# Second target for the scatter-adds: each slot's two blocks go to x_rows and y_rows, summed in the last graph stage

## What is computed

```python
x = x + _L0_gnn_ref(_layernorm(x), adj, W, b)       # A @ (ln @ W + b) / degree
x = x + _L0_ffn_ref(_layernorm(x)[None], ...)[0]    # 8 experts, top 2, 256 -> 1024 -> 256, gelu
x = x + _L1_gnn_ref(_layernorm(x), adj, W, b)       # relu(normalised (A + I) @ ln @ W.T + b)
x = x + _L1_ffn_ref(_layernorm(x)[None])[0]         # shifts of one-hot nibbles, elementwise per row
```

## Time and profile before

| what | value |
|---|---|
| median of 3 runs | 1076.81 us |
| the profiled execution's own time | 1077.18 us |
| its span on the core | 1075.2 us |
| PE busy | 956.4 us, 89% of the span |
| DVE / ACT / POOL busy | 559.4 / 404.4 / 360.0 us |
| second block, first work to last | 348.3 to about 794 us |
| last matmul of the second block, first of the third | 777.05 / 802.32 us |
| adds into `x_rows` (L1064) | 76, mean 1.604 us on POOL |
| read and written in memory | 176.41 and 22.94 MB |

### The profile page before, as it was taken

The page is one execution under the profiler, slowest core; times in us unless marked ns, Lnnn a source line. Parts: engine busy times, 40 slices in busy tenths (PEclk is TensorE's granted clock), DMA queues, the critical chain, the costliest instruction groups (busy, mean ns, idle before and its releaser), DMA issues. The chain is left out here.

```text
span 1075.2 us, 22179 instructions
## 1 busy us (share of the span) xinstructions
PE 956.4 (89%) x6724; PEld 627.4 (58%) x6725; DVE 559.4 (52%) x1643; ACT 404.4 (38%) x826; POOL 360.0 (33%) x416
## 2 busy tenths in 40 slices
PE   4988999999922799999999999999819999999993
PEld 1444544444411689898989898898704454444541
DVE  6734113127598566565656565665436334161754
ACT  4863758676787233232323232323112101010111
POOL 3510000014575345454545455454425320110110
PEclk9999999999965799999999999999959999999997
DMA  9785898899786423232332323232259978876771
GB/s 346 307 293 186 287 328 319 312 345 371 257 278 183 156 41 55 45 54 45 50 50 45 54 43 56 40 55 44 46 161 393 406 254 298 291 240 189 231 254 35
DMA packets 91265, 200.00 MB, mean 186 GB/s; under 512 B 13328, under 2 KB 47120, under 8 KB 91088
## 3 DMA queue, kind: packets, MB, share of 16 engines
q1 hardware_dynamic: 69248, 164.17, 43.5%
q0 software_dynamic: 17792, 31.02, 14.6%
q10 hardware_dynamic: 4176, 4.19, 1.2%
HBM read 176.41 MB, written 22.94 MB: 185 GB/s over the span
## 5 line engine op out<-in xcount | busy, mean ns | idle before, releaser
L921 PE MATMUL bank<-adj_f,feat 128*128 128x512 f16 x1024 | 240.8, 390 | 17.4 <-DMA adj_f<-in_adjT 15.7
L1202 ACT ACTIVATE act_f<-bank,b_sb 128x256 f32<-128x256 f32 x304 | 127.6, 471 | 288.4 <-PE bank L1148 288.4
L1148 PE MATMUL bank<-rT,experts 128*128 128x256 f16 x1824 | 207.8, 275 | 0.9 <-DVE rT L1215 0.9
L1169 PE MATMUL bank<-experts,act_h 128*128 x1824 | 205.3, 273 | 1.4 <-DVE y_f L1247 1.4
L1148 PEld LDWEIGHTS bank<-rT,experts 128*128 x1824 | 179.5, 98 | 22.9 <-issue 1.2
L1169 PEld LDWEIGHTS bank<-experts,act_h 128*128 128x128 f16 x1824 | 176.8, 98 | 21.6 <-issue 1.7
L1064 POOL DMA_INDIRECT x_rows<-y,token x76 | 121.9, 1604 | 193.1 <-DVE y L1254 165.2
L921 PEld LDWEIGHTS bank<-adj_f,feat 128*128 128x128 f16 x1024 | 97.5, 96 | 144.4 <-issue 18.1
L1588 PE MATMUL bank<-adj_g,feat 128*128 128x512 f16 x768 | 179.7, 387 | 0.3 <-POOL feat L1393 0.3
L805 ACT ACTIVATE spent<-adj_f 128x1024 f16<-128x1024 f32 x128 | 135.1, 1055 | 33.5 <-DMA adj_f<-in_adjT 28.3
L1588 PEld LDWEIGHTS bank<-adj_g,feat 128*128 128x128 f16 x768 | 73.8, 96 | 94.1 <-issue 0.8
(11 more groups left out here) (258 smaller groups left out, 910.0 us busy)
## 6 DMA issues: line engine op xcount, KB each, us to landing
adj_f<-in_adjT SPq DMA_DIRECT2D x128, 512.0 KB, 6.7
adj_g<-in_adjT SPq DMA_DIRECT2D x72, 512.0 KB, 6.0
adj_early<-in_adjT SPq DMA_DIRECT2D x24, 512.0 KB, 6.6
adj_g<-in_adjT SPq DMA_DIRECT2D x48, 256.0 KB, 3.1
unit_f<-in_W SPq DMA_DIRECT2D x16, 512.0 KB, 7.3
stage<-in_W SPq DMA_DIRECT2D x12, 512.0 KB, 7.0
x_ring<-in_x POOLq DMA_DIRECT2D x16, 256.0 KB, 7.6
x_rows<-agg SPq DMA_DIRECT2D x4, 1024.0 KB, 9.6
```

Of the source, the lines that this page charges most:

```text
L921: last = pe.matmul(mine(s)[ib * DC + c][:, :], feat0[:, j, h, c * P:(c + 1) * P], adj_0[j % RING][:, ib * HALF_SWEEP:(ib + 1) * HALF_SWEEP ...
L1148: last = pe.matmul(pb[2 + q][:, k * SLOT:(k + 1) * SLOT], w1_part(e * DC + (f // FQ * W2_UNIT0 + c), wh)[:, (f % FQ) * P:(f % FQ + 1) * P] ...
L1169: last = pe.matmul(pb[6 + r][:, 0:D], act_h[i][:, ah, f, r * P:(r + 1) * P], experts[:, ds(e * DC + (W2_UNIT0 + f // UH), 1), wh, (f % UH) ...
L1202: last = a.activation(act_f[q][:, k, :], pb[2 + q][:, k * SLOT:(k + 1) * SLOT], ACT.Gelu, bias=b1_sb[:, ds(e * FC + (2 * q + k), 1)], scal ...
```

## The change

The two blocks of a slot get a tensor each. Block 0 is added into `x_rows` as before, block 1 into a new tensor `y_rows`, which the first block fills with zeros (32 stores of 128 KB from `zeros_f`, a tile of zeros which takes the place of the unused `xn`). Each of the two has a semaphore of its own. Both adds of a slot are issued one behind the other, ahead of the gathers, and both are waited for at the end of the slot, before the next slot's adds. In the third block each piece is loaded from both tensors (y into a ring of 16 tiles, `y_ring`), and DVE adds y to x before the statistics.

```diff
@@ first block, SP
+            sp.wait_ge(sem("zrow_set"), 2)
+            for k in range(T // P):
+                sp.dma_start(y_rows[k * P:(k + 1) * P, :], zeros_f[:, :]).then_inc(sem("mix_stored"), 16)
             sp.wait_ge(sem("mix_ready"), 1)
             sp.dma_start(ln_rows[0:T, D:ROW].rearrange("(n p) d -> p n d", p=P), mix[:, :, :]
                          ).then_inc(sem("mix_stored"), 16)
...
-            sp.wait_ge(sem("mix_stored"), 16)
+            sp.wait_ge(sem("mix_stored"), 16 * (1 + T // P))
@@ first block, POOL
+            pool.memset(zeros_f[:, :], 0.0).then_inc(sem("zrow_set"), 1)
@@ second block, POOL
             def add_rows(i, r):
-                pool.indirect_dma_start(x_rows[:, :], ...
-                                        y[i][:, r, :], None, compute_op=ALU.add).then_inc(sem("landed"), 16)
+                pool.indirect_dma_start(sum_of[r][:, :], ...
+                                        y[i][:, r, :], None, compute_op=ALU.add).then_inc(sem(f"landed{r}"), 16)
-            def landed_until(s, r):
-                pool.wait_ge(sem("landed"), (s * SR + r) * 16 + 16)
+            def landed_until(s):
+                for r in range(SR):
+                    pool.wait_ge(sem(f"landed{r}"), s * 16 + 16)
                 pool.sem_inc(sem("waited"), 1)
...
                     add_rows(k, 0)
+                    add_rows(k, 1)
...
                     gather(k, token[k], AHEAD * SR)
-                    landed_until(s, 0)
-                    add_rows(k, 1)
                     pool.wait_ge(sem(f"rows_loaded{1 - k}"), (pr + (k + 2)) * (16 * SR))
                     take_tokens(s + 1, 1 - k)
-                    landed_until(s, 1)
+                    landed_until(s)
...
                 add_rows(k, 0)
-                landed_until(s, 0)
                 add_rows(k, 1)
...
-                landed_until(s, 1)
+                landed_until(s)
@@ third block, SP, load_x2
                 sp.dma_start(x_sb[:, at:at + tiles, :], x2_v[:, at:at + tiles, :]).then_inc(sem(f"x_loaded{g}"), 16)
+                k = at % (2 * G)
+                if at >= 2 * G:
+                    sp.wait_ge(sem("y_added"), at + tiles - 2 * G)
+                sp.dma_start(y_ring[:, k:k + tiles, :], y2_v[:, at:at + tiles, :]).then_inc(sem(f"x_loaded{g}"), 16)
@@ third block, DVE
-                v.wait_ge(sem(f"x_loaded{g}"), 32)
+                v.wait_ge(sem(f"x_loaded{g}"), 48)
+                for b in range(tiles):
+                    v.tensor_tensor(x_sb[:, at + b, :], x_sb[:, at + b, :], y_ring[:, (at + b) % (2 * G), :], ALU.add
+                                    ).then_inc(sem("y_added"), 1)
+                v.wait_ge(sem("y_added"), at + tiles)
```

More of the change, by code:

```diff
@@ L75, in program @@
     x_rows = nc.dram_tensor("x_rows", [T + P, D], F32, kind="Internal").ap()
+    y_rows = nc.dram_tensor("y_rows", [T + P, D], F32, kind="Internal").ap()
+    sum_of = (x_rows, y_rows)
     end = nc.sbuf_usable_end - 32
@@ L136, in program @@
     table = keep("table", [P, 64], I32)
-    xn = keep("xn", [P, 2, D], F32)
+    zeros_f = keep("zeros_f", [P, D], F32)
     WORK_AT = keep.at
@@ L1063, in add_rows @@
             def add_rows(i, r):
-                pool.indirect_dma_start(x_rows[:, :], bass.IndirectOffsetOnAxis(ap=token[i][:, r:r + 1], axis=0),
-                                        y[i][:, r, :], None, compute_op=ALU.add).then_inc(sem("landed"), 16)
-            def landed_until(s, r):
-                pool.wait_ge(sem("landed"), (s * SR + r) * 16 + 16)
+                pool.indirect_dma_start(sum_of[r][:, :], bass.IndirectOffsetOnAxis(ap=token[i][:, r:r + 1], axis=0),
+                                        y[i][:, r, :], None, compute_op=ALU.add).then_inc(sem(f"landed{r}"), 16)
+            def landed_until(s):
+                for r in range(SR):
+                    pool.wait_ge(sem(f"landed{r}"), s * 16 + 16)
                 pool.sem_inc(sem("waited"), 1)
@@ L1291, in program @@
     made = [w(f"made{i}", [P, G, D], F32) for i in range(2)]
+    y_ring = w("y_ring", [P, 2 * G, D], F32)
     factor = w("factor", [P, G], F32)
@@ L1315, in program @@
     x2_v = x_rows[0:T, :].rearrange("(n p) d -> p n d", p=P)
+    y2_v = y_rows[0:T, :].rearrange("(n p) d -> p n d", p=P)
     MARK, OP_SHL, OP_SHR, ALU_LO, OUTPUT_LO = 0, 39, 40, 64, 128
```

## The result

| what | before | after |
|---|---|---|
| median of 6 runs each | 1078.66 us | 1090.37 us |
| lowest and highest | 1073.89, 1080.23 | 1087.38, 1092.66 |
| the profiled execution's own time | 1077.18 us | 1089.53 us |
| its span | 1075.2 us | 1087.7 us |
| PE busy | 956.4 us | 960.0 us |

After over before is 1.0118, with a 95% interval from 1.010 to 1.0135: slower, by 12.5 us between the two spans, where +7.9 was forecast.

What follows compares the result with a forecast made beforehand. The prediction took PE to bound the expert loop, with waits bare behind it and POOL's feat holding PE in the last stage. 5.1 - 5.5 + 6.1 + 2.2 = +7.9 on 1077.18 gave 1085.1 us, range 1079.8 to 1089.8.

Steps and rivals of the forecast that it cites:

- Part 1: End of the first block: the zero stores on SP delay the mix store, +5.1 us.
- (f): First block's end: zero stores are bound by their issue; +4.8 us in all, 1082.0; chance 0.05.
- Part 2: Expert stage: nothing gained in the loop; at the tail, adds without the wait between save 5.5 us.
- the case priced at -4.8: Tail of the expert stage: POOL's hold-up on leaving the loop comes back whole, so the saving is 4.8 us.
- Part 3: Start of the last stage: second load and DVE's adds lengthen the chain to tile 8 by 6.1 us.
- Part 4: Last stage, tile 8: after 4.0 us idle PE restarts at half clock, +2.2 us.
- (a): Last stage: adds cost 0.25 us each on the chain and the clock holds; +3.7 us, 1080.9; chance 0.11.
- (g): Whole kernel faster: stores and adds both hidden, the tail gain alone left; 1071.7 us; chance 0.03.
- (b): Last stage, tile 8: the stall is as forecast but PE's clock holds; +5.7 us, 1082.9; chance 0.10.
- (c): Expert loop's exit: the hold-up costs what today's does, -2.4 for -5.5; +11.0 us, 1088.2; chance 0.10.
- (d): Last stage: doubled loads make adjacency tiles late for PE; +10.3 us, 1087.5; chance 0.08.
- (e): Paired adds: the second waits in the queue for the first; +13.4 us, 1090.6; chance 0.03.

Runs made afterwards that it cites:

- both paired kernels: Against the kernel before, both adds of a slot go into x_rows with no wait between: in all slots, ratio 0.9935; only in the last two, 0.9919.

## Why the prediction was off

The sign, the places and most prices were right; the sum was 4.6 us short of the spans' difference (12.5 less 7.9), and the time came out just above the range.

**Part 1, +6.1 for +5.1.** Mix landed 4.6 us behind its issue, at 353.35, where 353.1 had been forecast; 0.7 of the difference is hidden in the early start of this execution. The term that was too small is the 10.9 us for 4.19 MB: they took 11.8, which is 355 GB/s. The 385 came from a stretch elsewhere, where the row of this very stretch showed 353 and gave the +6.0 that stood as a bound. But the rows don't leave it to the rate alone. The DMA engines moved 380 GB/s from 339 to 345, close to the 385, and were no longer full from 347 on (0.83), while SP was still issuing stores, at 0.46 us each in the median and not 0.4. So rival (f), issue as the limit, had a part in the last stores; how the 0.9 us divide is open.

**Part 2, -4.9 for -5.5.** The loop's waits were free; both paired kernels and the changed one show it. At the tail the hold-up on leaving the loop came back, the case priced at -4.8. The kernel that pairs its adds behind the loop alone had none and saved 6.1. What holds POOL there isn't settled: the first wait behind the loop is long (4.16 and 4.31 us) where the loop itself pairs its adds, and was also long (4.09) before, and 3.70 with the unused tile, where the loop waits between them.

**Part 3, +10.2 for +6.1, the step that made the miss.** The step that failed is the price of an add on the chain, taken from rows in which POOL is idle, and with it the arrival of y's second piece. Three terms of its sum were too small:
- The eight adds of piece 2: 4.5 us and not 2.8. The price of 0.33 an add came from a row where DVE reads one tensor, and from additions behind the later sweeps, where POOL is idle. The chain's adds run while POOL splits the tiles that DVE has just scaled and works on the adjacency's tiles, and the runs show 0.46 to 0.56 each with POOL at work and 0.35 with POOL idle (3.71 to 4.50 and 2.77 for eight). The Trainium skill (SBUF — State Buffer, "Who interferes with whom") says that a DVE instruction with two SBUF inputs contends with a GpSimd instruction that reads SBUF, and calls the port pair that they share an exclusive lock. The traces here agree: single adds of 0.41 or 0.83 to 0.90 us, splits of 0.85 for 0.67, and one of 2.34 that sat out six adds.
- The six adds of piece 1: 3.04 us and not 2.1. The rows fit the same cause: in the run without loads, with no split under way when they began, they took 2.10.
- y's second piece: 1.9 us of waiting and not 0.4. I had taken 314 GB/s for the whole stretch from 795, and 0.75 us from the last byte to the landing. Windows of the changed kernel, then of the kernel before:

```profile
793.70:795.50 1.80, 0.00 (x0) 0.00 (x0) 1.01 (x4) 1.51 (x2) 1.05 (x3) 0.50 0.26 67
795.50:797.50 2.00, 0.00 (x0) 0.00 (x0) 1.73 (x12) 0.00 (x0) 0.00 (x0) 0.50 0.86 284
797.50:799.50 2.00, 0.00 (x0) 0.00 (x0) 1.84 (x9) 0.01 (x1) 0.00 (x0) 0.50 0.93 303
```

```profile
794.20:796.00 1.80, 0.00 (x0) 0.00 (x0) 1.01 (x4) 1.51 (x2) 1.05 (x3) 0.50 0.29 59
796.00:798.00 2.00, 0.00 (x0) 0.00 (x0) 1.72 (x13) 0.00 (x0) 0.00 (x0) 0.50 1.02 344
```

The slow first 1.8 us are in both kernels, and the forecast's average held them. Behind them the changed kernel moved 284 and 303 GB/s where the kernel before had 344; why isn't shown. The 2.10 MB were through 8.1 us after the stage's first work and not 7.5, and y's piece landed 1.7 us behind that, as the adjacency tiles queued behind it took a part of the bytes (0.8 us in the run that holds them back). The 0.75 doesn't follow from the forecast's own rows either: at 314 GB/s from 795 x1's last byte is at 798.3, and the landing at 799.4 is 1.1 behind it, which makes the wait 0.7 and not 0.4.

Together 0.9 + 1.7 + 1.5 = 4.1 us, all of the difference. My bound of 0.43 an add (3.4 for eight) didn't reach the 4.50 either: a bound from rows without contention bounds nothing where there is some.

**What PE did with it.** The stall at tile 2 was 4.2 us where 1.5 had been forecast, and the clock fell there, not at tile 8. That cost nothing: PE lost some 2 us between tiles 2 and 4 and stood idle for 3.4 at tile 8 anyway. Clock windows of the changed kernel (third number from the end):

```profile
809.00:810.00 1.00, 0.00 (x0) 0.00 (x0) 0.66 (x7) 0.21 (x1) 0.00 (x0) 1.00 1.09 350
810.00:811.00 1.00, 0.00 (x0) 0.00 (x0) 0.83 (x6) 0.00 (x0) 0.00 (x0) 0.68 1.10 349
811.00:817.00 6.00, 4.37 (x11) 1.58 (x12) 2.24 (x5) 1.94 (x5) 4.91 (x10) 0.50 1.06 387
```

**Part 4 and behind tile 8, +2.8 for +2.2, right by accident.** The clock at tile 8 held through 3.36 us of idle time (64 matmuls in 14.67 us), so the +2.2 priced there didn't come in this execution; in the run of adds alone it fell behind 4.92 us, and cost 1.8 (16.47). It fell too behind shorter idle times at the same tile, with the zeros on POOL and with the adds between the scalings:

```profile
826.97 16.03 PE L1603 MATMUL bank<-adj_g,feat 128*128 128x512 f16 x64 [2.77 <-POOL feat L1404]
831.72 16.27 PE L1614 MATMUL bank<-adj_g,feat 128*128 128x512 f16 x64 [3.18 <-POOL feat L1404]
```

So the term was sound in kind, and one trace doesn't tell how often it is paid (1.4 to 1.8 us where it was). Instead, "no further stall, nothing given back" failed: with piece 3's adds at 3.7 us and not 2.8, DVE needs 15.4 us for 8 tiles and PE 14.5, so PE waited at tiles 16 and 24, and the two stretches of 8 tiles took 1.8 us more than before. The last 1.0 us is behind the last sweep. Windows of the changed kernel, then of the kernel before:

```profile
1069.00:1072.00 3.00, 2.95 (x18) 2.21 (x19) 1.30 (x3) 0.00 (x0) 0.00 (x0) 0.63 0.00 0
```

```profile
1057.50:1060.50 3.00, 2.79 (x24) 2.27 (x24) 1.84 (x5) 0.00 (x0) 0.00 (x0) 1.00 0.00 0
```

Both come behind the same 2.01 us of idle time. The clock fell in the one and held in the other; it fell too in the kernel with the unused tile, and held in that with adds alone. With the same work and the same idle time on both sides, I don't count it as the change's.

**The rivals.** (a) and (g) are out: adds cost more than 0.33, not less, and neither stores nor adds were hidden. (b)'s mechanism, the clock that holds at tile 8, is what the profiled execution shows; its time, 1082.9, was missed by the other terms. (c) came in the size that part 2 had named, 4.8. (d), late adjacency tiles, shows only where there are no adds (1.45 us); its own sum was off too, since 15.2 MB at 314 GB/s end at 843.4 and land 0.75 later, which makes +9.7 and not +10.3. (e) is out although its 1090.6 is the nearest to the measured 1090.37: it has no gain at the tail, and the tail gained 4.9 us. (f) had a part in part 1, in the other direction: the stores' issue came on top.

## What to carry to other kernels

Take the price of an instruction from a row in which the engines that will run beside it are at work; here an add with two SBUF inputs on DVE took 0.46 to 0.56 us beside a POOL at work and 0.35 beside an idle one, and POOL paid in turn. A wait that protects against two writers of one row was better removed by giving the rows that can coincide places of their own (0.9935) than by a second tensor, which must be cleared, loaded and added (1.0118). And a wait hidden by PE in a loop may be bare behind it: only the last two slots' waits were worth anything here, 5 to 6 us.

## What the runs showed that I had not expected

- **Idle time alone doesn't say whether PE's clock falls.** It held through 3.36 us (changed kernel, tile 8, 48 matmuls after the last stall), fell behind 2.77 and 3.18 us at the same tile (zeros on POOL, adds between the scalings), and fell in 2.24 us (loads alone, tile 2, 16 matmuls after a stall of 20 us). Behind 2.01 us, in the same work, it did one or the other from run to run.
- **An unused tile of 4 bytes a partition moved the time by -0.24%** (0.9976, interval 0.9964 to 0.9989), with matmuls of 128x512 shorter by 0.7% (14.56 and 14.66 us for 64). Which tile's place does it wasn't tried.
- **The stage's first loads are slow.** In the first 1.8 us they moved 67 GB/s in the changed kernel and 59 before, with a DMA share of 0.26 and 0.29. With y's loads among them the next 4 us moved 284 and 303, and 341 to 418 came only behind that; without them it was 344 at once.
